# Mixture-of-experts FFN on one core: GpSimd drains inside the program, SyncE waits for the last scatters, fewer branches on TensorE, and b2's load moved

## The reference, cut to what matters

```
x: (2, 1024, 256) f32, cond_8: (2, 8), D = 256, H = 1024, E = G = 8
w_bot[b] = sum_g cond_8[b, g] * (weight[g] * mask)            # one 256x256 matrix per batch
c        = x @ w_bot[b].T + bias                               # 2048 token rows
top1     = argmax(c @ gate_w.T + gate_b)                       # one expert per token
y[t]     = relu(c[t] @ w1[e].T + b1[e]) @ w2[e].T + b2[e],  e = top1[t]
out      = x + y
```

## Time and profile before

| | |
|---|---|
| runs of the kernel before | median 177.32 us of 3 (176.75 to 179.02) |
| the profiled execution's own time | 177.17 us |
| its span (first to last instruction) | 174.8 us, so 2.4 us lie around it |
| busy, share of the span | PE 90%, PEld 76%, DVE 69%, ACT 61%, POOL 35% |
| granted TensorE clock | 0.989 of full speed over the span |
| chain that ended last | PE 57%, DMA 21%, issue 10%, DVE 3% |

### The profile page before, as it was taken

One profiled execution on the slowest core, in us unless ns is written; L12 is line 12 of the kernel. 1 busy time (PEld: TensorE's weight loads), 2 busy tenths in 40 slices (PEclk: granted clock), 3 DMA queues, 4 the chain that ended last, 5 costly groups with the idle time before them and its releaser, 6 DMA issues.

```text
span 174.8 us, 6097 instructions
## 1 busy us (share of the span) xinstructions
PE 156.8 (90%) x1807; PEld 133.3 (76%) x1807; DVE 120.8 (69%) x225; ACT 106.7 (61%) x192; POOL 61.9 (35%) x59
## 2 busy tenths in 40 slices
PE   5999899994799999998978999999999999999720
PEld 2347588642689999997867999999999898888610
DVE  0496899957999979899999748989753543644000
ACT  3505988121899799699966578899536563453000
POOL 8200000058850226265187545662244220122220
PEclk9999999999999999999999999999999999999995
DMA  3999999957977889899978813222220100100000
GB/s 67 353 410 409 414 401 380 313 166 247 339 211 271 224 287 330 290 311 332 326 269 251 287 33 118 52 75 64 90 67 21 50 22 11 37 30 30 19 20 0
DMA packets 13791, 33.35 MB, mean 191 GB/s; under 512 B 2619, under 2 KB 6843, under 8 KB 13632
## 3 DMA queue, kind: packets, MB, share of 16 engines
q1 hardware_dynamic: 8288, 24.39, 40.1%
q0 software_dynamic: 2688, 6.30, 10.7%
q10 hardware_dynamic: 2784, 2.26, 3.9%
HBM read 30.06 MB, written 6.95 MB: 212 GB/s over the span
## 4 chain that ended last, share of the span: by engine, by line
PE 57%; DMA 21%; issue 10%; DVE 3%; DVEq 2%; POOL 1%; ACT 1%; SPq 1%; POOLq 0%; ACTq 0%
PE psum L913 22%; PE psum L897 18%; DMA wsp<-w_all 16%; PE psum L797 6%; PE psum L833 4%; PE psum L824 3%; DMA rows_in<-both_rows,tok_of_slot 2%; DMA both_rows<-stage 2%; PE psum L885 1%; DVE wsp L610 1%; PE psum L810 1%; PE psum L781 1%; DVE hT L718 1%; DVEq L610 1%; SPq L326 1%
## 5 line engine op out<-in xcount | busy, mean ns | idle before, releaser
L897 PE MATMUL psum<-xs,stage 128*128 128x128 f16 x1008 | 59.7, 219 | 2.2 <-ACT psum L509 1.1
L913 PE MATMUL psum<-wsp,hT 128*128 x504 | 58.5, 273 | 3.0 <-DVE hT L718 1.4
L897 PEld LDWEIGHTS psum<-xs,stage 128*128 128x128 f16 x1008 | 57.6, 98 | 3.8 <-issue 2.5
L913 PEld LDWEIGHTS psum<-wsp,hT 128*128 128x128 f16 x504 | 47.9, 98 | 10.1 <-issue 4.7
L413 POOL DMA_INDIRECT out<-rows_in,tok_of_slot x17 | 23.1, 1360 | 55.5 <-DVE rows_in L723 52.3
L408 POOL DMA_INDIRECT rows_in<-both_rows,tok_of_slot x17 | 25.2, 1480 | 39.7 <-issue 35.5
L610 DVE SCALAR_TENSOR_TENSOR wsp<-wsp x28 | 32.9, 1221 | 4.5 <-ACT wsp L492 4.3
L718 DVE SCALAR_TENSOR_TENSOR hT<-psum,hT 128x512 f16<-128x512 f32 x42 | 27.1, 683 | 11.7 <-ACT hT L526 11.7
L509 ACT ACTIVATE psum<-b_col 128x1024 f32 x21 | 21.5, 1023 | 16.3 <-issue 13.2
L492 ACT ACTIVATE wsp<-wsp x28 | 27.9, 1060 | 3.0 <-issue 2.6
L526 ACT ACTIVATE hT<-psum 128x512 f16<-128x512 f32 x42 | 22.7, 588 | 4.3 <-PE psum L897 4.2
(11 more groups left out here) (105 smaller groups left out, 99.4 us busy)
## 6 DMA issues: line engine op xcount, KB each, us to landing
wsp<-w_all SPq DMA_DIRECT2D x32, 512.0 KB
wsp<-cond_w SPq DMA_DIRECT2D x4, 512.0 KB, 6.8
wsp<-x_t SPq DMA_DIRECT2D x2, 1024.0 KB, 10.7
both_rows<-x_rows ACTq DMA_DIRECT2D x2, 1024.0 KB, 13.6
b_all<-b SPq DMA_DIRECT2D x1, 1024.0 KB, 17.4
both_rows<-stage SPq DMA_DIRECT2D x1, 768.0 KB, 7.0
both_rows<-stage SPq DMA_DIRECT2D x1, 512.0 KB, 5.8
both_rows<-stage SPq DMA_DIRECT2D x1, 384.0 KB, 4.6
```

What stands on the lines that cost most here:

```text
L897: last = t_.matmul(o, w1s[:, b, w:w + P], xs[:, b, xp, k * P:(k + 1) * P], start=False, stop=(c % 4 == 3 and k == KD - 1 and wp == 1), ski ...
L913: last = t_.matmul(ps_y[b], hT[:, b, hp, c * P:(c + 1) * P], w, start=False, stop=(c == KH - 1 and w is low), skip_group_check=True)
```

## The change

Four edits. GpSimd executes `drain()` before scatters 9, 12, 14 and 15 and before every scatter from 16 on; its waits for the last scatters are gone. SyncE, when its chunks are done, loads the number of tiles and waits for the `stored` semaphores of tiles 8 to 15 and, in nested conditions, of tiles 16 and up. TensorE's conditions are written anew: one condition for a tile from 15 on instead of three, and the last tile's layer 1, layer 2 of the tile before and its own layer 2 stand in one block without a branch between. The 1 MB load of b2 moves behind the wait for gather 0, ahead of chunk 6. GpSimd's waits ahead of the first gather also change places.

```diff
--- before.py
+++ after.py
@@ -58,6 +58,7 @@
 WSCALE = 64.0
 RING = 8
 OWN_SLOTS = 6
+DRAINS = (9, 12, 14, 15)
 HALF = KH * P // 2
 SURE = TOK // P
 STORES = ((0, 6), (6, 10), (10, 13), (13, 15), (15, 16))
@@ -302,9 +303,9 @@
         def load_used(eng):
             return eng.value_load(tiles_used[0:1, 1:2], min_val=SURE, max_val=SLOT_TILES)
 
-        def slot_tiles(eng, tile, plans=True):
-
-            plan = plans and Plan(eng, 0)
+        def slot_tiles(eng, tile):
+
+            plan = Plan(eng, 0)
             for i in range(SLOT_TILES):
                 plan = tile(i, i % 2, i % RING, i // RING + 1, plan)
 
@@ -339,7 +340,6 @@
 
             for q in range(CPE):
                 load_chunk(0, q)
-            sp.dma_start(b2_all[:, :, :], b2.partition_broadcast(P)).then_inc(ld_b2, 16)
             for q in range(CPE):
                 confirm(q, 1)
             for n in range(len(STORES)):
@@ -352,6 +352,7 @@
             load_chunk(1, 0)
             load_chunk(1, 1)
             sp.wait_ge(x_in[0], 16)
+            sp.dma_start(b2_all[:, :, :], b2.partition_broadcast(P)).then_inc(ld_b2, 16)
             load_chunk(1, 2)
             sp.wait_ge(x_in[1], 16)
             load_chunk(1, 3)
@@ -372,6 +373,20 @@
                 if q + IN_FLIGHT < CPE:
                     load_chunk(E - 1, q + IN_FLIGHT)
 
+            def all_stored(i):
+                if i < SLOT_TILES:
+                    with sp.If(used > i):
+                        sp.wait_ge(stored[i % RING], 16 * (i // RING + 1))
+                        all_stored(i + 1)
+                    with sp.Else():
+                        sp.nop()
+
+            sp.wait_ge(experts_known, 1)
+            used = load_used(sp)
+            for i in range(SURE - RING, SURE):
+                sp.wait_ge(stored[i % RING], 16 * (i // RING + 1))
+            all_stored(SURE)
+
         @block.gpsimd
         def _(pool):
             g = nc.gpsimd
@@ -409,25 +424,27 @@
                                      bounds_check=TOK - 1, oob_is_err=False).then_inc(x_in[i % RING], 16)
 
             def scatter(i):
+                if i >= SURE:
+                    pool.drain()
                 pool.wait_ge(y_ready, i + 1)
                 g.indirect_dma_start(out, token(i), res(i % RING), None,
                                      bounds_check=TOK - 1, oob_is_err=False).then_inc(stored[i % RING], 16)
 
             pool.wait_ge(pool_step, 3)
+            pool.wait_ge(x_stored, 32)
+            pool.wait_ge(routed, 1)
             for n in range(len(STORES)):
                 pool.wait_ge(rows_stored[n], 16)
-            pool.wait_ge(routed, 1)
-            pool.wait_ge(x_stored, 32)
             for i in range(RING):
                 gather(i)
             pool.wait_ge(experts_known, 1)
             used = load_used(pool)
             for i in range(SLOT_TILES):
+                if i in DRAINS:
+                    pool.drain()
                 if_used(pool, used, i, lambda: scatter(i))
                 if i >= 1:
                     if_used(pool, used, i + RING - 1, lambda: gather(i + RING - 1))
-            for i in range(SURE - RING, SLOT_TILES):
-                if_used(pool, used, i, lambda: pool.wait_ge(stored[i % RING], 16 * (i // RING + 1)))
 
         @block.scalar
         def _(act):
@@ -919,15 +936,28 @@
             turn_x(0, 0, 0, 1)
             keep_clock_up(4)
 
-            def tile(i, b, r, turn, plan=None):
-                if_used(pe, used, i + 1, lambda: turn_x(i + 1, 1 - b, (r + 1) % RING, turn + (1 if r == RING - 1 else 0)))
-                if_used(pe, used, i, lambda: layer1(i, b))
-                if late(i, 1):
-                    if_used(pe, used, i - 1, lambda: layer2(i - 1, 1 - b))
-
-            slot_tiles(pe, tile, plans=False)
-            i = SLOT_TILES - 1
-            if_used(pe, used, i, lambda: layer2(i, i % 2))
+            def turn_next(i):
+                turn_x(i + 1, (i + 1) % 2, (i + 1) % RING, (i + 1) // RING + 1)
+
+            def last_tile(i):
+
+                layer1(i, i % 2)
+                layer2(i - 1, (i - 1) % 2)
+                layer2(i, i % 2)
+
+            for i in range(SURE - 1):
+                turn_next(i)
+                layer1(i, i % 2)
+                if i >= 1:
+                    layer2(i - 1, (i - 1) % 2)
+            for i in range(SURE - 1, SLOT_TILES - 1):
+                with pe.If(used > i + 1):
+                    turn_next(i)
+                    layer1(i, i % 2)
+                    layer2(i - 1, (i - 1) % 2)
+                with pe.Else():
+                    if_used(pe, used, i, lambda: last_tile(i))
+            if_used(pe, used, SLOT_TILES - 1, lambda: last_tile(SLOT_TILES - 1))
 
 
 def kernel(x, cond_8, L0_cond_weight, L0_cond_mask, L0_cond_bias, L0_ffn_gate_w, L0_ffn_gate_b,
```

## The result

| | before | changed |
|---|---|---|
| median of the runs | 177.28 us of 4 | 183.97 us of 4 (182.16 to 185.75) |
| ratio to before | | 1.032, 95% interval 1.022 to 1.043 |
| profiled execution, its span | 177.17, 174.8 | 184.88, 182.7 |
| span's mean granted TensorE clock | 0.989 | 0.975 |

The account below looks back on a forecast made before the run. Bound by a chain of waits: row stores to first gathers, TensorE alone from about 94 us, GpSimd's DRAIN at the end. Gains 0.8 + 1.1 + 1.1 + 3.6 = 6.6 us gave 170.7 us, range 169.3 to 174.3.

Parts of the forecast that it names:

- TensorE, last tile ... the four branches: TensorE before the last layer 2: removing four branches ends 1.16 us of idleness; gain 1.1 us, bounds 0.6 and 1.16.
- TensorE, conditions of tiles 15 to 20: TensorE's late tiles: one condition instead of three saves two thirds of 1.65 us; gain 1.1 us, bounds 0 and 1.65.
- Rival 4: Gains of TensorE or the weights' stream given back, by b2's delay or the last tile's far jump: 173.1 us; chance 0.08.
- The end of the block: After the last scatter: SyncE waits, GpSimd's final DRAIN is short, end 0.5 us after landing; gain 3.6 us, bounds 0 and 3.9.
- work per DMA: GpSimd's DRAIN: its length read from two rows as 0.08 us for each DMA before it.
- a drain behind one DMA: GpSimd's late drains before scatters: 0.3 us each, with 1 us free before the scatter of tile 20.
- rival 2: GpSimd from tile 14: each drain waits for its scatter's landing, then takes 3.5 us; slower, 187.8 us, chance 0.07.
- b2: Moving b2's load out of the front starts layer 1 of tile 0 earlier; gain 0.8 us, bounds 0 and 1.7.
- The rest of the lead is a wait elsewhere: Front: gathers start 1.7 us earlier, but layer 1 of tile 0 only 0.75 at most; the remainder becomes waiting.

Follow-up runs that it names:

- pe_only: The kernel before with only the changed kernel's new TensorE conditions: 184.25 us, ratio 1.034.
- pe_nested: The kernel before with the changed TensorE code, nested so that copies for a last tile lie behind all tiles that go on: 179.54 us, ratio 1.003.
- no_pe: The changed kernel with TensorE's conditions as before, keeping drains, SyncE's waits and b2's move: 175.99 us, ratio 0.987.
- tail_only: The changed kernel without b2's move and with the TensorE code of before: 174.94 us, ratio 0.982.
- b2_only: The kernel before with only b2's load moved behind gather 0: 178.73 us, ratio 1.002.
- pad_real: The kernel before with about 240 never-run TensorE instructions in an Else that five late tiles jump over: 186.04 us, ratio 1.045.
- sp_only: The kernel before with SyncE instead of GpSimd waiting for the last stores, no drain in mid-program: 176.19 us, ratio 0.989.

## Why the prediction was wrong, step by step

**The step that failed: "TensorE, last tile ... the four branches", with "TensorE, conditions of tiles 15 to 20".** I counted branches and took their price from the rows of before, 65 to 307 ns. I asked where a new branch jumps to for the last tile alone, as a rival, and not for the tiles that go on or the way out. The diff shows it: whoever takes the If runs past an Else with a layer 1 and two layers 2, and the last tile jumps over an If with a whole tile's code. In before nobody jumps over more than one layer on this path. The sum had +2.2 us of gain; the runs show a loss of 6.1 (`pe_only`, 3.4%).

The gain that I had counted does exist. In `pe_nested` layer 2 starts come 5.52 us apart (133.00 to 155.08 in four tiles), against 5.84: as in the early tiles, so the upper bound of that term and not two thirds of it. The idle time before the last layer 2 went from 1.16 to 0.17 us: 1.0 for my 1.1. What failed is not the size of what is removed but the price of what is added, which was not in the sum at all.

**Rival 4 was the right mechanism, at 2.4 us where the runs show 8.3** (2.2 forecast as gain, 6.1 lost). The one far jump that it named, the last tile's, came: a pause of 3.12 us and 1.63 of lower clock behind it, where the rival had a DMA's landing of 2.4 us and no clock. What it did not have are the jumps of the tiles that go on over their Else (3.77 us of pauses and 1.63 of clock) and the way out of the code. Its argument against, that no row is over 307 ns "also where it jumps over a layer 1", was true of those rows and did not bear on jumps over 170 or 235 instructions. The rule of the Trainium skill in "Runtime: NRT & Kernel Launch", section "Instruction fetch mechanics", that a taken branch beyond the code held forces a fetch, is borne out by this case's runs: branch rows of 1.5 to 3.6 us, and 23 instruction packets of 16 KB in the changed kernel where before had 17. What decides whether a jump of this length stalls is not shown: in the changed kernel two of the five over an Else did not. I gave it 8 chances in 100 because no row showed it; but no row could have, since before has no such jump. Absence of a row is evidence only where the thing could have shown.

**The end of the block: right in size, wrong in one price.** Without the new TensorE code the end comes 3.6 us sooner, as forecast (`no_pe`, `tail_only`). The work per DMA was read rightly from two rows (0.08; three rows now give 0.083). But I costed a drain behind one DMA at 0.3 us, and it takes 2.1 to 2.5: it ends 0.08 us after that DMA has landed. So rival 2's first half was true, the drain does wait for the landing. Its second half was not, since most of the work runs beside the landing, though not all of it. The drain ahead of scatter 9 has 25 DMAs behind it:

```profile
L444 POOLq DRAIN  x1: 5641/5641/5641, 105.2 to 105.2; - x1
```

The last of the 25, a gather, starts at 106.25, is generated at 107.3 and has landed at 109.7. The drain ends at 110.8: 1.1 us after the landing, and 3.5 us after the generation, where the price per DMA makes 2.1. With 6 and 4 DMAs behind it a drain of that trace ended 0.29 and 0.21 us after the last landing, so that some 0.04 us for each DMA stand behind the landing. In `no_pe` the waits cost nothing. In the changed kernel the drain ahead of the last scatter took 4.45 us, and held it up by 2.7.

**TensorE's way out of its code.** The sum left TensorE out once its last matrix product is done. In the changed kernel it was busy for 6.8 us more with leaving its code, in two jumps of 3.57 and 3.23, which is as long as all of the end of the block. Even with a short drain ahead of the last scatter the changed kernel would have ended there.

**b2.** The lead (1.07 us at the first layer 1, forecast 0.75 at most) came, the gain did not (1.002, 0.997 to 1.006). The sum had 0.8 for it. "The rest of the lead is a wait elsewhere" holds for all of it: a megabyte that is moved behind is still ahead of something. Which wait takes it back over the runs of `b2_only` stays open: its one profile, of the fastest execution of twelve (176.28 us), kept a lead of 0.8 us up to the last scatter.

**The range did not follow from its bounds.** The four upper bounds (1.7, 1.65, 1.16 and 3.9) add up to 8.4 us, which is 168.9 and not 169.3, and the lower ones to 0.6, which is 176.7 and not 172.5. That was not what failed: no term had a loss as its lower bound, so no sum of them could have reached 184.

## What to carry to other kernels

Cost a branch by what lies between it and its target, in instructions, and put code that almost never runs where the frequent path need not jump over it: on TensorE 68 instructions were free, and 170 to 240 cost a pause of up to 3.1 us at most of the jumps, at times with a lower clock behind it. Count the way out of the code as well; it can be the last thing that ends. And a GpSimd drain should stand once, late, where GpSimd is idle until the landing of its last DMA and some 0.04 us for each DMA behind that, or for 0.083 us for each DMA from the last generation on, whichever ends later; what it does there the end of the program need not do.

## What had not been expected of the hardware

- A stall for code can fall in the middle of straight code: in `pad_real` 2.0 us after 18 of a layer 1's 48 products, 1.5 us behind the jump's row.
- TensorE also crawled where it had not jumped far, in the profiled execution of `no_pe` only one product or two in each 0.7 us for 2.5 us, and similarly in `sp_only`'s at 103 to 107 us. The traces of before, `pe_only` and `b2_only` don't have it. Its cause is open:

```profile
114.80 0.27 PE psum L914 x2
115.07 0.50 issue
```

- A scatter lands in 16 parts. Of the last seven scatters in each of the 14 traces (98), in 93 the last part landed within 0.1 us of the fifteenth. In the five others it was 0.2 to 2.1 us behind, three of them in the changed kernel's execution, and each time one of TensorE's instruction packets was under way within that scatter's time; others overlapped such a packet and lost nothing. That the two collide was not tried. It is what made the drain ahead of the last scatter 4.45 us, and a drain turns such a late part into a late scatter.
